# A fused graph-layer kernel: node work one step later behind the edges, SyncE's queue reordered, window loads signalled per half

## The chip, the cores and the metric

The kernel runs on one core of a Trainium2 chip. TensorE (PE), VectorE (DVE), ScalarE (ACT) and GpSimd (POOL) compute; SyncE (SP) only issues transfers and reads registers. GpSimd also issues the gathers, whose addresses come from an index tile. The metric is the device time of one execution in microseconds. The kernel before took 705.6 us (median of 3 runs, 704.37 to 707.84).

## The reference

One message-passing layer over 50,000 nodes of 128 features and 25,000 edges that are sorted by their destination:

```
h   = relu(layernorm(x))                                   # 50000 x 128
e   = [h[src], h[dst], edge_attr(32), vec[src], vec[dst]]  # 25000 x 290
msg = silu(e @ mW1 + mb1) @ mW2 + mb2                      # 25000 x 128
agg = segment_sum(msg, dst)                                # 50000 x 128
u   = silu([h, agg, vec] @ uW1 + ub1) @ uW2 + ub2
out = x + layernorm(h + u) * gamma + beta
```

## The kernel before

**Two streams in one pipeline.** The edges are worked in 49 steps of 512 (four tiles of 128), the nodes in 49 steps of 1,024 (eight tiles of 128). `run_pipeline` lets every engine walk the same list of steps; in step n an engine does its part for edges near n and for nodes near n minus `NODE_LAG` (4). Steps 0 to 3 therefore hold edge work only (with the first loads and norms of nodes), steps 4 to 48 hold both, steps 49 to 52 the last four node steps, and steps 53 and 54 finish them. `it.edge(d)` and `it.node(d)` name the edge or node step that lies d steps off. Each engine executes its own instructions in the written order; semaphores order the engines among each other.

**Edges.** GpSimd gathers the two end rows of each edge of step n (line 418, eight gathers). VectorE takes their statistics (lines 897 and 898) and computes reciprocal deviations in a chain of small operations that ends in `rstd` and `minus`. One step later ScalarE normalises the gathered rows (`norm_ends`, line 611), TensorE turns them (line 530), ScalarE copies them out (line 666), and the two coordinates of each edge are turned on TensorE (line 499), copied (line 627) and moved into `feat_t` by SyncE (line 326). Another step later TensorE sums the hidden layer (lines 487, 488, 491), ScalarE applies silu (line 619), TensorE makes the message (517, 519), ScalarE evicts it (line 643) and SyncE stores it to the tensor `msgs` in HBM (line 360).

**Nodes.** The messages of 128 nodes are a short run of rows of `msgs`, since edges are sorted. SyncE reads the first edge of each of the eight node tiles from SBUF into a register (line 351, eight reads per step) and loads a window of 112 message rows for each tile (line 376, eight loads into `msg_in`), one step ahead of their use. VectorE compares each message's destination with the node numbers and so makes a 0/1 matrix `match` (line 798, in two halves), TensorE multiplies windows by `match` into the hidden layer (line 555), ScalarE applies silu (line 697), TensorE makes the update (567, 569), VectorE takes its statistics (849), centres it (782) and two steps after the match finishes the output (813), which SyncE stores (line 342). GpSimd adds `beta` to six of eight tiles of x (line 438), and waits with that for the match of the step.

**What the window loads need.** Before them SyncE waits until a message store has landed: with a lag of 4 it is `it.edge(2 - NODE_LAG)` = `it.edge(-2)`, the very store that SyncE issued earlier in the same step (line 374). All eight loads raise one semaphore, and the first half of `match` waits for all eight.

**SyncE's order in a step** is: register reads, x load, message store, coordinates, edge indices and edge attributes (every other step), the node coordinate row, output store, window loads.

The flag `sorted_near` picks this path (`WHOLE`) on the chip; the other path, for edges that are not sorted, is not run on these inputs.

## Time and profile before

| | |
|---|---|
| median of 3 runs | 705.6 us (704.37 to 707.84) |
| profiled execution, its own time | 707.65 us |
| its span in the trace | 705.6 us |
| DVE busy | 624.5 us, 89% |
| PE busy | 613.4 us, 87% |
| ACT busy | 542.4 us, 77% |
| POOL busy | 470.8 us, 67% |
| TensorE's granted clock | 0.986 of full speed over the span |
| moved by the DMA engines | 119.07 MB, 169 GB/s |

The table's busy times are averages over stages. SyncE has no busy time in such a table: its register reads and transfer issues are not counted, and are seen only in its timeline and in the chain of waits. The run has three stages: edge steps alone (to about 60 us), 45 steps that hold both kinds of work, and node steps alone (from about 650 us).

### The profile page before, as it was taken

The numbers are of one execution on the slowest core, as the hardware profiler recorded it, in microseconds if no ns is written. First come the engines' busy times: TensorE is split into PE (matmuls) and PEld (weight loads), VectorE is DVE, ScalarE is ACT, GpSimd is POOL, SyncE is SP. The second block draws the span as 40 slices with busy tenths as digits, with TensorE's granted clock in tenths as the row PEclk, the third lists the DMA queues.
The fourth block names the chain that finished last, engine by engine and source line by source line (L and its number), as shares of the span: only waits on it lengthen the run. The fifth ranks groups of instructions, "written<-read, shape, count | busy, mean of one in ns | idle before, by whom it ended". The sixth has DMA issues, their size and how long they took to land.

```text
span 705.6 us, 17834 instructions
## 1 busy us (share of the span) xinstructions
PE 613.4 (87%) x3685; PEld 446.7 (63%) x3732; DVE 624.5 (89%) x2949; ACT 542.4 (77%) x1181; POOL 470.8 (67%) x447
## 2 busy tenths in 40 slices
PE   1478899999899899899899899899899899989972
PEld 0155676676676676676676676676676676666662
DVE  5564789989999999999999999999999999988887
ACT  1388887887888888888888888888887888888720
POOL 7775777777777677677777677677777677763200
PEclk9999999999999999999999999999999999999997
DMA  5535576566577666667577577576576577664332
GB/s 145 171 109 133 133 217 178 163 205 160 160 186 190 167 185 191 166 186 196 155 192 197 155 200 193 150 207 186 149 215 179 148 213 181 179 191 124 122 91 84
DMA packets 91988, 119.07 MB, mean 169 GB/s; under 512 B 20250, under 2 KB 65493, under 8 KB 91944
## 3 DMA queue, kind: packets, MB, share of 16 engines
q1 hardware_dynamic: 77684, 91.61, 44.1%
q0 software_dynamic: 12752, 26.57, 17.0%
q10 hardware_dynamic: 1508, 0.42, 0.3%
q8 instruction: 13, 0.21, 0.1%
q14 instruction: 31, 0.25, 0.1%
HBM read 79.63 MB, written 38.70 MB: 168 GB/s over the span
## 4 chain that ended last, share of the span: by engine, by line
SPq 44%; DMA 17%; issue 16%; DVE 10%; PE 5%; POOL 2%; ACT 2%; DVEq 0%; POOLq 0%; ACTq 0%
SPq L376 19%; DMA msgs<-msg 14%; SPq L351 14%; SPq L326 3%; DVE y_out L813 2%; SPq L334 2%; POOL ends_in L418 2%; DVE stats L849 2%; DMA ends_in<-in_rows,end_idx 1%; SPq L360 1%; DVE centred L782 1%; DMA msg_in<-msgs 1%; SPq L342 1%; DVE stats L839 1%; SPq L319 1%
## 5 line engine op out<-in xcount | busy, mean ns | idle before, releaser
L418 POOL DMA_INDIRECT ends_in<-in_rows,end_idx x392 | 382.4, 976 | 116.2 <-issue 105.1
L611 ACT ACTIVATE ends_norm<-ends_in,minus,rstd 128x128 f32<-128x128 f32 x392 | 155.6, 481 | 11.5 <-DVE minus L954 11.5
L555 PEld LDWEIGHTS ps_hid<-match,msg_in 113*128 113x128 f32 x784 | 99.1, 191 | 102.4 <-DVE match L798 77.4
L611 ACT ACTIVATE x_norm<-x_in,minus,rstd 128x128 f32<-128x128 f32 x392 | 155.5, 482 | 0.0
L555 PE MATMUL ps_hid<-match,msg_in 113*128 113x128 f32 x784 | 108.0, 281 | 39.2 <-DVE match L798 39.2
L438 POOL TENSOR_TENSOR x_beta<-x_in,beta_row 128x768 f32<-128x768 f32 x47 | 85.5, 1819 | 79.9 <-DVE match L798 58.5
L813 DVE SCALAR_TENSOR_TENSOR y_out<-centred,rstd,x_beta 128x128 f32<-128x128 f32 x392 | 128.4, 336 | 2.1 <-issue 0.3
L849 DVE BATCH_NORM_STATS2 stats<-ps_upd 128x6 f32<-128x128 f32 x392 | 110.0, 289 | 2.6 <-issue 2.6
L567 PE MATMUL ps_upd<-w_out,hidden_n 128*128 128x128 f32 x784 | 105.2, 278 | 5.2 <-DVE centred L782 5.2
L782 DVE SCALAR_TENSOR_TENSOR centred<-ps_upd,y_mean,gamma_row 128x128 f32<-128x128 f32 x392 | 107.4, 341 | 0.0
L798 DVE SCALAR_TENSOR_TENSOR match<-iota_sb,const_sb,msg_in 112x512 f32<-112x512 f32 x98 | 72.7, 750 | 39.2 <-DMA msg_in<-msgs 38.7
L839 DVE BATCH_NORM_STATS2 stats<-x_in 128x6 f32<-128x128 f32 x392 | 102.1, 284 | 0.8 <-DVE s_sq L925 0.2
L552 PE MATMUL ps_hid<-h_t,w_node 128*128 128x512 f32 x196 | 101.0, 597 | 0.0
L567 PEld LDWEIGHTS ps_upd<-w_out,hidden_n 128*128 128x128 f32 x784 | 96.5, 194 | 6.0 <-DVE centred L782 6.0
L697 ACT ACTIVATE hidden_n<-ps_hid,node_bias 128x512 f32<-128x512 f32 x98 | 65.2, 679 | 31.3 <-PE ps_hid L555 31.2
L619 ACT ACTIVATE hidden_e<-ps_e,mb_col 128x512 f32<-128x512 f32 x49 | 33.7, 688 | 63.4 <-PE ps_e L491 62.1
L897 DVE BATCH_NORM_STATS2 stats<-ends_in 128x6 f32<-128x128 f32 x196 | 54.5, 278 | 20.2 <-DMA ends_in<-in_rows,end_idx 20.1
L635 ACT ACTIVATE h_t<-ps_t,b_col 128x1024 f32<-128x1024 f32 x49 | 54.6, 1115 | 15.4 <-PE ps_t L509 11.8
L530 PE MATMUL ps_t<-const_sb,ends_norm 128*128 128x128 f32 x392 | 54.1, 283 | 10.3 <-ACT ends_norm L611 10.0
L569 PE MATMUL ps_upd<-const_sb,h_t 128*128 128x128 f32 x392 | 59.3, 274 | 0.0
L491 PE MATMUL ps_e<-feat_t,w_feat 34*128 34x512 f32 x98 | 55.9, 651 | 3.3 <-DMA feat_t<-coords 3.3
L666 ACT ACTIVATE ends_t<-ps_t 128x1024 f32<-128x1024 f32 x49 | 50.2, 1025 | 10.4 <-PE ps_t L530 10.1
(90 smaller groups left out, 789.4 us busy)
## 6 DMA issues: line engine op xcount, KB each, us to landing
x_in<-in_x_steps SPq DMA_DIRECT2D x49, 512.0 KB
out<-y_out SPq DMA_DIRECT2D x48, 512.0 KB
msg_in<-msgs SPq DMA_DIRECT2D x392, 56.4 KB
msgs<-msg SPq DMA_DIRECT2D x49, 258.0 KB
ends_in<-in_rows,end_idx POOLq DMA_INDIRECT x392
feat_t<-in_attr SPq DMA_DIRECT2D x25, 128.0 KB
feat_t<-coords SPq DMA_DIRECT2D x98, 2.0 KB
match<-in_node_vec SPq DMA_DIRECT2D x49, 4.0 KB
```

The lines of the kernel that those rows point to most:

```text
L351: firsts = [sp.value_load(first_edge[0:1, bass.ds(N_TILES * soon.n + j, 1)]) for j in range(N_TILES)]
L376: sp.dma_start(msg_in[soon.half][0:WINDOW, j, :], msgs[bass.ds(firsts[j], WINDOW), :]).then_inc(msg_loaded[soon.half], 16)
L418: nc.gpsimd.indirect_dma_start(out=dst, out_offset=None, in_=rows, in_offset=bass.IndirectOffsetOnAxis(ap=end_idx[s.slot // 2][:, s.slot % ...
L438: nc.gpsimd.tensor_tensor(x_beta[later.slot][:, 0:POOL_TILES, :], x_in[later.slot][:, 0:POOL_TILES, :], beta_row[:, :, :].broadcast_to([P, ...
L552: nc.tensor.matmul(ps_hid[:, bank], w_node[:, :], h_t[k.half][:, bank], start=True, stop=False)
L555: last = nc.tensor.matmul(ps_hid[:, cols(j)], msg_in[k.half][0:WINDOW + 1, j, 0:H], match[k.half][0:WINDOW + 1, j, :], start=False, stop=j ...
L567: nc.tensor.matmul(ps_upd[:, cols(j)], hidden_n[:, cols(j)], w_out[:, :], start=j == tiles[0], stop=False)
L611: return nc.scalar.activation(dst, source, function, bias=minus[was][:, c:c + 1], scale=rstd[was][:, c:c + 1])
L782: last = V.scalar_tensor_tensor(centred[:, j, :], ps_upd[:, j * P:(j + 1) * P], y_mean[:, j:j + 1], gamma_row[:, 0, :], ALU.subtract, ALU. ...
L813: last = V.scalar_tensor_tensor(y_out[done.half][:, j, :], centred[:, j, :], rstd[was][:, Y_AT + j:Y_AT + j + 1], x_beta[done.slot][:, j, ...
L839: last = V.bn_stats(stats[:, X_AT + j, :], x_in[n.slot][:, j, :])
L849: last = V.bn_stats(stats[:, Y_AT + j, :], ps_upd[:, j * P:(j + 1) * P])
```

## The change

`NODE_LAG` becomes 5. There is so one more step with edges alone at the start, 44 steps with both in place of 45, and one more node step behind the last edges. The awaited store is now `it.edge(-3)`, issued one step earlier.

In SyncE's list a step with node work runs: coordinates, message store, coordinate row, register reads, window loads, x load, edge indices and attributes, output store. A step without node work runs: x load, coordinates, indices and attributes, register reads, message store, row, window loads.

The window loads raise one semaphore for the first four tiles and another for the last four, and each half of `match` waits for its own.

In the steps without node work PE turns the coordinates before the hidden sum, and ACT copies the coordinates and applies silu before it normalises the ends. ACT executes one small silu on a spare column at the start. DVE splits the bias after the first step's statistics and takes the first x statistics ahead of the gathered ones; GpSimd's first `x_beta` no longer waits for a match.

```
-NODE_LAG = 4
+NODE_LAG = 5
...
-            def body(it):
-                soon, done, e = it.node(1), it.node(-2), it.edge(-2)
-                if soon and it.mode == WHOLE:
...
-                    firsts = [sp.value_load(first_edge[0:1, bass.ds(N_TILES * soon.n + j, 1)]) for j in range(N_TILES)]
...
+                def load_windows(firsts):
...
+                        if past := it.edge(2 - NODE_LAG):
+                            wait_apart(sp, msg_stored[past.slot], 16 * (past.fills4 + 1), sp_passed)
+                        for j in range(N_TILES):
+                            sp.dma_start(msg_in[soon.half][0:WINDOW, j, :], msgs[bass.ds(firsts[j], WINDOW), :]).then_inc(
+                                msg_loaded[soon.half][2 * j // N_TILES], 16)
...
+                if not k:
+                    load_ahead()
+                    if own:
+                        move_coords(own)
+                    load_pairs()
+                    firsts = find_windows()
+                    store_messages()
+                    load_row()
+                    load_windows(firsts)
+                else:
+                    if own:
+                        move_coords(own)
+                    store_messages()
+                    load_row()
+                    load_windows(find_windows())
+                    load_ahead()
+                    load_pairs()
...
-                    wait(pool, match_ready, 2 * later.n - 2)
+                    if isinstance(later.n, int) and later.n == 2:
+                        pool.wait_ge(x_beta_low_ready, 2)
+                    else:
+                        wait(pool, match_ready, 2 * later.n - 2)
...
+            act.wait_ge(fold_loaded, 16 * N_FOLD)
+            nc.scalar.activation(spare[:, :], mb2_col[:, :], ACT.Silu)
...
                 if not k:
+                    copy_coords()
+                    activate_edges()
                     norm_ends()
-                    activate_edges()
-                    copy_coords()
                     copy_ends()
...
+                    if it.mode == WHOLE:
+                        dve.wait_ge(msg_loaded[k.half][half], 16 * HALF * (k.fills2 + 1))
                     if half == 0:
-                        if it.mode == WHOLE:
-                            dve.wait_ge(msg_loaded[k.half], 16 * N_TILES * (k.fills2 + 1))
```

SyncE's queue around one even step, in the kernel before: from the last window load of a step to the first of the next.

```order
L376 DMA msg_in<-msgs 112x129
L351 TENSOR_LOAD first_edge x8
L334 DMA x_in<-in_x_steps 128x1024
L360 DMA msgs<-msg 128x516
L326 DMA feat_t<-coords 1x4x128 x2
L314 DMA end_idx<-in_ends 128x16
L319 DMA feat_t<-in_attr 32x1024
L369 DMA match<-in_node_vec 1x1024
L342 DMA out<-y_out 128x1024
L376 ISA
```

The same piece of SyncE's queue in the changed kernel (one of the first steps, which has no output to store yet).

```order
L392 DMA msg_in<-msgs 112x129
L337 DMA x_in<-in_x_steps 128x1024
L317 DMA end_idx<-in_ends 128x16
L322 DMA feat_t<-in_attr 32x1024
L329 DMA feat_t<-coords 1x4x128 x2
L368 DMA msgs<-msg 128x516
L374 DMA match<-in_node_vec 1x1024
L383 TENSOR_LOAD first_edge x8
L392 ISA
```

The x load, the indices, the attributes and (from two steps later on) the output store have moved behind the windows; coordinates and message store are first, and the register reads stand right before the window loads.

ScalarE's queue in the third step, which has edge work alone, in the kernel before.

```order
L651 ACTIVATE msg<-end_idx 128x4
L611 ACTIVATE ends_norm<-ends_in,minus,rstd 128x128 x8
L619 ACT_TABLE_LOAD
L619 ACTIVATE hidden_e<-ps_e,mb_col 128x512
L627 ACTIVATE coords<-ps_f 8x128
L666 ACTIVATE ends_t<-ps_t 128x1024
L643 ACTIVATE msg<-ps_e 128x4x128
```

The same step on ScalarE in the changed kernel.

```order
L669 ACTIVATE coords<-ps_f 8x128
L661 ACTIVATE hidden_e<-ps_e,mb_col 128x512
L693 ACTIVATE msg<-end_idx 128x4
L653 ACTIVATE ends_norm<-ends_in,minus,rstd 128x128 x8
L708 ACTIVATE ends_t<-ps_t 128x1024
L685 ACTIVATE msg<-ps_e 128x4x128
```

Coordinates and the hidden layer's silu stand ahead of the eight norms, and the table load is gone from here to the program's start.

## Rows read from the trace of the kernel before

**Rows 1.** The page: the chain of work that ended last, shares of span.

```profile
SPq 44%; DMA 17%; issue 16%; DVE 10%; PE 5%; POOL 2%; ACT 2%; DVEq 0%; POOLq 0%; ACTq 0%
```

**Rows 2.** Timeline, SyncE, two steps: start us, us, engine line, op, out<-in, count.

```profile
300.05 0.35 SPq L334 DMA_DIRECT2D x_in<-in_x_steps  x1
...
313.36 0.35 SPq L334 DMA_DIRECT2D x_in<-in_x_steps  x1
...
316.83 0.37 SPq L342 DMA_DIRECT2D out<-y_out  x1
318.61 3.87 SPq L376 DMA_DIRECT2D msg_in<-msgs  x8
326.10 0.35 SPq L334 DMA_DIRECT2D x_in<-in_x_steps  x1
```

**Rows 3.** Waits of the SP queue, 169 to 550 us: total us, times, longest.

```profile
SPq L72 <- DMA msgs<-msg: 13.9, 14, 1.6
```

**Rows 4.** Waits of all engines, 169 to 550 us.

```profile
PE ps_hid L555 <- DVE match L798: 26.0, 29, 1.4
DVE match L798 <- DMA msg_in<-msgs: 14.6, 25, 1.2
```

**Rows 5.** Timeline, VectorE's match: step 4 (both halves), steps 5 and 48 (second).

```profile
60.85 1.41 DVE L798 SCALAR_TENSOR_TENSOR match<-iota_sb,const_sb,msg_in 112x512 f32<-112x512 f32 x2 [8.29 <-DMA msg_in<-msgs]
...
73.61 0.74 DVE L798 SCALAR_TENSOR_TENSOR match<-iota_sb,const_sb,msg_in 112x512 f32<-112x512 f32 x1
...
640.04 0.74 DVE L798 SCALAR_TENSOR_TENSOR match<-iota_sb,const_sb,msg_in 112x512 f32<-112x512 f32 x1
```

**Rows 6.** Timeline, ScalarE, from one silu of the edges to the next.

```profile
637.09 0.69 ACT L619 ACTIVATE hidden_e<-ps_e,mb_col 128x512 f32<-128x512 f32 x1 [1.34 <-PE ps_e L491]
...
639.87 3.18 ACT L611 ACTIVATE ends_norm<-ends_in,minus,rstd 128x128 f32<-128x128 f32 x8
...
649.66 0.69 ACT L619 ACTIVATE hidden_e<-ps_e,mb_col 128x512 f32<-128x512 f32 x1 [1.34 <-PE ps_e L491]
```

**Rows 7.** Timeline, TensorE, the same step.

```profile
643.10 1.09 PE L530 MATMUL ps_t<-const_sb,ends_norm 128*128 128x128 f32 x8
```

**Rows 8.** Timeline, GpSimd, one step.

```profile
313.20 1.82 POOL L438 TENSOR_TENSOR x_beta<-x_in,beta_row 128x768 f32<-128x768 f32 x1 [1.37 <-DVE match L798]
...
324.19 0.95 POOL L418 DMA_INDIRECT ends_in<-in_rows,end_idx  x1 [0.30 <-DVE y_out L813]
```

**Rows 9.** Timeline, VectorE, from the ends' statistics to the next match.

```profile
315.11 0.28 DVE L897 BATCH_NORM_STATS2 stats<-ends_in 128x6 f32<-128x128 f32 x1
...
325.12 0.75 DVE L798 SCALAR_TENSOR_TENSOR match<-iota_sb,const_sb,msg_in 112x512 f32<-112x512 f32 x1
```

**Rows 10.** DMA queues (q0 gathers), 326 to 326.5 us: packets, MB, share.

```profile
q0 software_dynamic: 19, 0.01, 11.1%
```

**Rows 11.** The chain in order of time: start us, us, what.

```profile
58.76 2.07 DMA msg_in<-msgs
...
73.49 4.96 DMA ends_in<-in_rows,end_idx
...
99.71 5.30 DMA ends_in<-in_rows,end_idx
```

**Rows 12.** DMA queues (q1 is SyncE's), 104 to 105 us.

```profile
q1 hardware_dynamic: 102, 0.37, 94.1%
```

**Rows 13.** Timeline, ScalarE, the table load and step 4's message eviction.

```profile
36.36 1.28 ACT L619 ACT_TABLE_LOAD   x1
...
59.52 0.60 ACT L643 ACTIVATE msg<-ps_e 128x512 f32<-128x512 f32 x1 [1.02 <-PE ps_e L519]
```

**Rows 14.** Timeline, VectorE, node steps behind the last edges.

```profile
674.33 1.41 DVE L798 SCALAR_TENSOR_TENSOR match<-iota_sb,const_sb,msg_in 112x512 f32<-112x512 f32 x2 [3.16 <-DMA msg_in<-msgs]
...
683.01 1.42 DVE L798 SCALAR_TENSOR_TENSOR match<-iota_sb,const_sb,msg_in 112x512 f32<-112x512 f32 x2
...
691.88 2.19 DVE L813 SCALAR_TENSOR_TENSOR y_out<-centred,rstd,x_beta 128x128 f32<-128x128 f32 x8
```

More of the change, by code:

```diff
@@ L344, in body, with load_ahead, load_pairs, store_messages @@
             def body(it):
-                soon, done, e = it.node(1), it.node(-2), it.edge(-2)
-                if soon and it.mode == WHOLE:
+                soon, k, done, e, own = it.node(1), it.node(0), it.node(-2), it.edge(-2), it.edge(-1)
+                def load_ahead():
+                    if further := it.node(5):
+                        if it.begins_nodes():
+                            for n in range(further.n):
+                                load_nodes(Step(n, n, 0))
+                        load_nodes(further)
+                def load_pairs():
+                    if (s := it.edge(2)) and s.slot % 2 == 0:
+                        load_edges(s)
+                    if (s := it.edge(0)) and s.slot % 2 == 0:
+                        load_attr(s)
+                def store_messages():
+                    if not e:
+                        return
+                    wait_apart(sp, dst_copied, e.n + 1, sp_passed)
+                    wait_apart(sp, msg_ready, e.n + 1, sp_passed)
+                    sp.dma_start(msgs_v[e.n], msg[e.slot][:, :, :]).then_inc(msg_stored[e.slot], 16)
+                def load_row():
+                    if not soon:
+                        return
+                    wait_apart(sp, hidden_n_summed, 2 * soon.n - 2, sp_passed)
+                    sp.dma_start(match[soon.half][WINDOW:WINDOW + 1, :, :], coord_v[soon.n]).then_inc(coord_loaded[soon.half], 16)
+                def find_windows():
+                    if not soon or it.mode != WHOLE:
+                        return None
                     if isinstance(soon.n, int) and soon.n == 0:
@@ L361, in body @@
-                if s := it.edge(-1):
-                    move_coords(s)
-                if (s := it.edge(2)) and s.slot % 2 == 0:
-                    load_edges(s)
-                if (s := it.edge(0)) and s.slot % 2 == 0:
-                    load_attr(s)
-                if soon:
-                    wait_apart(sp, hidden_n_summed, 2 * soon.n - 2, sp_passed)
-                    sp.dma_start(match[soon.half][WINDOW:WINDOW + 1, :, :], coord_v[soon.n]).then_inc(coord_loaded[soon.half], 16)
-                if done and e:
-                    store_nodes(done)
@@ L372, in body @@
-                if soon and it.mode == WHOLE:
-                    if past := it.edge(2 - NODE_LAG):
-                        wait_apart(sp, msg_stored[past.slot], 16 * (past.fills4 + 1), sp_passed)
-                    for j in range(N_TILES):
-                        sp.dma_start(msg_in[soon.half][0:WINDOW, j, :], msgs[bass.ds(firsts[j], WINDOW), :]).then_inc(msg_loaded[soon.half], 16)
-                elif soon:
+                    return [sp.value_load(first_edge[0:1, bass.ds(N_TILES * soon.n + j, 1)]) for j in range(N_TILES)]
@@ L380, in body @@
                     sp.dma_start(agg_in[soon.half][:, :, :], table_v[soon.n]).then_inc(agg_loaded[soon.half], 16)
-                if done and not e:
+                if not k:
[15 more added lines that the diff above has]
+                    load_pairs()
+                if done:
                     if isinstance(done.n, int) and done.n == NODE_STEPS - 1:
@@ L893, in body @@
                         centre(j)
+                if nxt and it.begins_nodes():
+                    for j in range(N_TILES):
+                        x_stat(nxt, j)
                 if new:
@@ L899, in body @@
                     last.then_inc(ends_stats, 1)
-                if nxt and it.begins_nodes():
-                    for j in range(N_TILES):
-                        x_stat(nxt, j)
                 if not (new or nxt or prev):
```

63 lines of the change are left out of this document (32 added, 31 removed).

## The prediction

> **What bounds the kernel now.** The page's busy times come first and mislead: VectorE at 89% and TensorE at 87% look like the bound. The chain of work that ended last says otherwise: 44% of the span lies in SyncE's own queue and 17% in transfers, only 10% on VectorE [rows 1]. So I read SyncE's timeline. From one x load to the next it takes 13.31 us in an even step (300.05 to 313.36) and 12.74 us in an odd one (313.36 to 326.10) [rows 2]. In the even step every gap is a few hundredths of a microsecond: the queue is simply full. In the odd step, which has no index and attribute loads, the output store ends at 317.20 and the first window load comes at 318.61 [rows 2]. About 0.37 us of such a gap is register work (the same place in the even step); the other 1.04 us is the wait for the message store of the same step to land. Over 169 to 550 us, 29 steps, that wait sums to 13.9 us in 14 odd steps [rows 3].
>
> Who waits for SyncE: VectorE waits for the windows 14.6 us in these 29 steps, and TensorE waits 26.0 us for VectorE's match behind it [rows 4]. From step 5 to step 48 the second half of match moves from 73.61 to 640.04 us, 43 intervals of 13.17 us [rows 5].
>
> What a step would take without that wait, loop by loop:
> - SyncE: 381 us less 13.9 us over 29 steps is 12.66 us. Its steps alternate, 13.31 us and 12.74 - 1.04 = 11.70 us in the two shown.
> - VectorE: 381/29 = 13.14 us less 14.6/29 = 0.50 us is 12.64 us, at most.
> - ScalarE with TensorE: silu of the edges starts at 637.09, the eight norms of the ends run from 639.87 to 643.05, TensorE's transposes start at 643.10 directly behind them, and the next silu starts at 649.66 [rows 6, 7]. That ring closes in 12.57 us with no wait for a match in it, and the change leaves its order alone.
> - The gathers: GpSimd adds beta once the match is done (313.20), and issues the last of eight gathers at 324.19 [rows 8]. The last packets of the gather queue pass between 326 and 326.5 us [rows 10], 2.31 us behind that issue. VectorE needs 10.76 us from the ends' statistics to the end of the next match (315.11 to 325.87) [rows 9]. This ring spans two steps: 10.99 + 2.31 + 10.76 + 0.1 = 24.2 us, 12.1 us a step.
>
> So four rings lie at 12.1 to 12.7 us, and the kernel runs at 13.17. That is the room.
>
> **The change part by part.**
>
> *Lag 5.* The awaited store is a step older, so it was issued some 12 us before, and the slowest landing fits many times: the wait of 13.9 us in 29 steps goes. What is late next is SyncE's own list, 12.66 us, with the ScalarE ring 0.1 us under it. Rings so close add up their small disturbances, and SyncE's even steps are 0.65 us over its mean, which is covered only while the windows are early enough. I take 12.75 us. The ends are 12.57 us (the ScalarE ring alone) and 13.6 us (the gather rival below).
>
> *SyncE's new order.* Nothing is added: eight register reads, eight window loads, one x load, one store, two coordinate moves, one row and one output store per step, as before. Moved past other work are the x load (512 KB), the indices, the attributes and the output store (512 KB): they start some 8 us later against the message store. The x load has time, since VectorE reads it more than a step later. The indices are needed for the gathers of two steps later; this margin shrinks by about 5 us and I cost it at nothing, hidden by GpSimd's wait for the match; without that cover it would be some 0.5 us a step. The windows no longer queue behind 512 KB of output, worth something only where they are late. What the moved megabyte meets is the gathers' end: the slow rival.
>
> *Semaphore per half.* The first match may start four window issues earlier, half of 3.87 us [rows 2]; the second half still waits for the last. In a full pipeline VectorE's 12.64 us hides that. I count it only in the first and last steps.
>
> *The head.* The first match comes one step later, at step 5, so I compare it with step 5 before, at 73.61 us [rows 5]. It needs windows whose issue now stands behind the store of message 2, evicted in step 4. Before, this eviction ended at 60.12 [rows 13]; ScalarE's eight norms (3.18 us [rows 6]) now stand ahead of it, so 63.3. Then store and row 1.0 us, eight window loads with gaps 4.6 us, landing 2.07 us [rows 11], and 0.4 us to the second half: 71.4 us, 2.2 us less than before. Earlier statistics, the bias split behind them and GpSimd's first addition, which sat 5.6 us for a match, serve the same start. Bounds: -6 us (most of the 8.29 us that VectorE waits here [rows 5]) to +3 us.
>
> *The table load.* It takes 1.28 us between two activations of the third step [rows 13] and goes to a time when ScalarE idles; that is inside the head's bounds. The Trainium skill (ScalarE: Activation LUTs, "What ACT_TABLE_LOAD costs") gives a switch some 2.66 us with a drain; here silu follows the load at once, so the trace shows the load's 1.28 us and no drain. By the page the head would be 1.4 us shorter.
>
> *The tail.* Before, from step 48's match (640.04) to the end are 65.6 us. A node step alone takes 8.7 us (674.33 to 683.01) where VectorE waits for nothing, and 12 us where it waits 3.16 us for windows [rows 14]. Now: 12.4 us from match 48 to 49 (this step still takes x statistics), 8.2 to step 50, 10.5 to step 51 (its windows stand behind the last message store), 8.9, 8.7, then 8.2 to the output work of step 54, 7.5 for one more, 6.2 to the end as before: 70.6 us, 5.0 us more. Bounds: +1 to +8.7 us, a whole step.
>
> *Sum.* 71.4 + 43 x 12.75 (548.3) + 70.6 = 690.3 us of span, against 705.6. The profiled execution took 707.65 us, 2.05 us around its span; with the same 2.05 the changed one takes 692.3, 15.3 us less. The median before was 705.6, so I predict 690 us.
>
> **The rivals.**
>
> *R1, it stops only at the ScalarE ring.* Then 43 x 12.57 = 540.5 us, and 682 us in all. For it: 12.57 us was reached late in the run [rows 6]. Against: SyncE's mean of 12.66 us is instruction work that stays.
>
> *R2, slower: the gathers land late.* Twice early in the run the last gather took 4.96 and 5.30 us to land [rows 11], in place of 2.31. At the second, SyncE's queue held the DMA engines at 94.1% from 104 to 105 us [rows 12], while the mid-run gather lands in a quiet spell [rows 10]. The new order lets x load and output store start right behind the windows, 8 to 10 us after a match, and the last gather is issued 12 us after it. If they meet in every step, the two-step ring is 10.99 + 4.96 + 10.76 + 0.1 = 26.8 us, 13.4 a step, with 5.30 us 13.6: 43 x 13.43 + 71.4 + 70.6 = 719 us. It decides where the landing passes 3.6 us (two steps of 12.75); above 4.3 us the gain is gone. Against it: if this ring slows the kernel, SyncE is no longer the bound, is up to 3 us earlier, and its megabyte is over before the gathers end. The Trainium skill (DMA: Bandwidth & Descriptors, "Queues, rings and completion order") says that each DMA engine takes turns between the queues that hold work, a packet at a time; the 94.1% beside a late gather agrees. By it alone the cost of a meeting is bounded by the share, so it makes a later landing likely and a stopped one not.
>
> *R3, the gain is eaten.* Landings of 4 us or window issues that stretch (4.64 us is the kind seen at the start) hold a step at 13.05 us: 561 + 142 = 703 us. For it: rings this close. Against: the same queue did 3.87 us per eight windows in most steps.
>
> *R4, the wait does not go.* Excluded but for an error of reading, 1 in 50: 708 us, with the tail's cost alone.
>
> **How the numbers follow.** Forecast (685 to 698 us) 0.62, R1 0.17, R3 0.10, R2 0.09, R4 0.02. A difference of 0.5%, 3.5 us, is about what a measurement of this kernel can tell from none. Faster than 702 us are the forecast, R1 and four tenths of R3: 0.83. Within 0.5%: most of R3's rest, R4's edge: 0.08. Slower: 0.09. The range runs from 678 us (R1 with the head's good end) to 705 us (R3 whole); outside are R2, R4 and a sliver below.
>
> **What would show it.** In SyncE's timeline the gap before the windows is gone in odd steps and a pair of steps takes 25.3 to 25.5 us. Match to match 12.75 us; VectorE's wait for windows under 0.2 us a step. The ScalarE ring shows TensorE's transposes waiting for the norms. The first match at step 5 near 71 us, the last two-sided match near 620, 70 us before the end. I am wrong if VectorE's statistics wait for gathers in the middle of the run (R2), if SyncE's pair stays at 26 us (R3 or R4), or if the tail takes more than 75 us.

## The result: 0.9% slower, where 2% faster was forecast

The changed kernel takes 714.22 us (median of 12 runs, 709.62 to 716.56) beside 707.69 us for the kernel before (12 runs, 704.37 to 708.99): ratio 1.0087, 95% interval 1.0065 to 1.011. It lies outside the range of 678 to 705 us. The profiled execution took 712.72 us, its span is 710.8.

Cut at the same two places as the forecast, the second half of match of step 5 and of step 48:

| part of the span, us | before | forecast | after |
|---|---|---|---|
| head, to match of step 5 | 73.61 | 71.4 | 78.93 |
| 43 steps, one step | 566.4 (13.17) | 548.3 (12.75) | 556.9 (12.95) |
| tail | 65.6 | 70.6 | 74.9 |
| span | 705.6 | 690.3 | 710.8 |

Against before: +5.3 - 9.5 + 9.4 = +5.2 us. Against the forecast every part is worse: +7.5, +8.6, +4.3.

The page of after, busy times and the chain that ended last (it answers to [rows 1], where 44% lay in SyncE's queue):

```profile
PE 620.7 (87%) x3685; PEld 452.2 (64%) x3732; DVE 627.1 (88%) x2962; ACT 540.4 (76%) x1181; POOL 469.8 (66%) x447
DVE 29%; issue 24%; POOL 22%; PE 10%; DMA 7%; ACT 5%; SPq 2%; DVEq 1%; POOLq 0%; ACTq 0%
```

SyncE went from 44% to 2%. The bound has moved, as meant, and to VectorE and GpSimd's gathers. SyncE's timeline of after (start us, us), one step from x load to x load, against [rows 2]:

```profile
399.94 0.35 SPq L337 DMA_DIRECT2D x_in<-in_x_steps  x1
400.62 0.37 SPq L345 DMA_DIRECT2D out<-y_out  x1
401.26 1.56 SPq L329 DMA_DIRECT2D feat_t<-coords  x2
403.25 0.36 SPq L368 DMA_DIRECT2D msgs<-msg  x1
403.95 0.28 SPq L374 DMA_DIRECT2D match<-in_node_vec  x1
407.79 3.86 SPq L392 DMA_DIRECT2D msg_in<-msgs  x8
412.03 0.35 SPq L337 DMA_DIRECT2D x_in<-in_x_steps  x1
```

What SyncE waits for most between 169 and 550 us, against [rows 3] (us in total, times, longest):

```profile
SPq L72 <- ACT msg L685: 1.3, 5, 0.3
```

and what VectorE waits for most in the same stretch, against [rows 4]:

```profile
DVE stats L943 <- DMA ends_in<-in_rows,end_idx: 7.2, 8, 1.5
```

The wait for the message store (13.9 us) is gone, and so is VectorE's for the windows (14.6 us). New is VectorE's wait for gathered rows. The two matches that bound the middle, against [rows 5]:

```profile
78.93 0.75 DVE L841 SCALAR_TENSOR_TENSOR match<-iota_sb,const_sb,msg_in 112x512 f32<-112x512 f32 x1 [1.09 <-DMA msg_in<-msgs]
...
635.86 0.74 DVE L841 SCALAR_TENSOR_TENSOR match<-iota_sb,const_sb,msg_in 112x512 f32<-112x512 f32 x1
```

**The head.** ScalarE in step 3 of after and into step 4:

```profile
49.56 3.17 ACT L653 ACTIVATE ends_norm<-ends_in,minus,rstd 128x128 f32<-128x128 f32 x8
54.79 1.02 ACT L708 ACTIVATE ends_t<-ps_t 128x1024 f32<-128x1024 f32 x1 [2.06 <-PE ps_t L568]
56.92 0.60 ACT L685 ACTIVATE msg<-ps_e 128x512 f32<-128x512 f32 x1 [1.11 <-PE ps_e L557]
...
62.51 0.69 ACT L661 ACTIVATE hidden_e<-ps_e,mb_col 128x512 f32<-128x512 f32 x1 [1.77 <-PE ps_e L529]
```

and TensorE beside it:

```profile
52.78 1.97 PE L568 MATMUL ps_t<-const_sb,ends_norm 128*128 128x128 f32 x8 [3.95 <-ACT ends_norm L653]
54.97 1.92 PE L557 MATMUL ps_e<-w_fold,hidden_e 128*128 128x128 f32 x8 [0.22 <-issue]
...
57.67 2.05 PE L525 MATMUL ps_e<-ends_t,w_src 128*128 128x512 f32 x2 [0.56 <-ACT msg L685]
59.51 1.91 PE L526 MATMUL ps_e<-ends_t,w_dst 128*128 128x512 f32 x2
61.35 1.12 PE L529 MATMUL ps_e<-feat_t,w_feat 34*128 34x512 f32 x2
```

Read as a ring: norms (49.56), transposes (52.78), the sums of the message, which stand behind the transposes on TensorE (54.97), the eviction of the message (56.92), the next hidden sum, which is made in the same tile `ps_e` and waits for that eviction (57.67 to 62.47), silu (62.51), and only then, since silu now stands ahead of them on ScalarE, the next norms. They start at 63.19, 13.6 us after the last. ScalarE's copy of the transposed rows (54.79 to 55.81) is not a link of this ring: it ended 1.9 us before the hidden sum began, although the expectation of old_head below names it as one.

The first four silus of the edges (steps 2 to 5) are 13.6, 13.6 and 13.6 us apart in after, and 9.6, 9.0 and 14.7 us in the kernel before: 7.6 us more in these three steps. The same work is longer here than in the full pipeline (transposes 1.97 us, 1.09 in [rows 7]), since the granted clock is at its lower level for most of this time. Windows of 5 us in after, the columns being length, busy times, granted clock, DMA share and GB/s:

```profile
35.00:40.00 5.00, 1.05 (x5) 0.85 (x5) 4.39 (x28) 3.85 (x10) 3.78 (x5) 0.75 0.34 82
40.00:45.00 5.00, 4.44 (x17) 3.32 (x16) 0.23 (x2) 1.77 (x3) 3.78 (x5) 0.50 0.25 59
```

and in before:

```profile
35.00:40.00 5.00, 3.58 (x15) 3.09 (x16) 3.76 (x23) 4.39 (x8) 3.78 (x5) 1.00 0.23 53
40.00:45.00 5.00, 2.42 (x8) 0.95 (x6) 2.00 (x9) 4.49 (x13) 4.09 (x4) 1.00 0.46 107
```

TensorE was busy 1.05 of 5 us ahead of a stretch at 0.50 (1.2 GHz) in after; in before 3.58 of 5, and the clock stayed at 1.00 (2.4 GHz). So the ring idles the engine, and what follows runs at the lower clock. The clock is not what makes the head late, though: windows_first, with the old order and a head 11 us shorter, also has a stretch at 0.50 (45 to 50 us). What the clock adds to the ring was not measured by itself.

**The meeting of transfers.** In the step shown above x load and output store go out at 399.94 and 400.62. The last gather is issued at 402.44. Windows of 1 us show the DMA engines full behind it:

```profile
404.00:405.00 1.00, 1.00 (x8) 0.76 (x7) 1.00 (x5) 1.00 (x4) 0.83 (x1) 1.00 1.01 400
405.00:406.00 1.00, 1.00 (x8) 0.76 (x8) 1.00 (x5) 1.00 (x4) 0.99 (x1) 1.00 0.75 289
```

the chain gives that gather's landing

```profile
402.44 4.65 DMA ends_in<-in_rows,end_idx
```

and VectorE is late by 0.95 us:

```profile
407.11 0.29 DVE L943 BATCH_NORM_STATS2 stats<-ends_in 128x6 f32<-128x128 f32 x1 [0.95 <-DMA ends_in<-in_rows,end_idx]
```

In [rows 8, 10] the last packets passed 2.31 us behind the issue, in a quiet spell; by its semaphore, as here, that gather landed 2.51 us behind it.

**The tail.** SyncE of after, behind the last edge step,

```profile
661.36 0.37 SPq L368 DMA_DIRECT2D msgs<-msg  x1
661.83 0.30 SPq L374 DMA_DIRECT2D match<-in_node_vec  x1
665.58 4.13 SPq L392 DMA_DIRECT2D msg_in<-msgs  x8
```

and VectorE's match that waits for these windows:

```profile
669.18 0.75 DVE L841 SCALAR_TENSOR_TENSOR match<-iota_sb,const_sb,msg_in 112x512 f32<-112x512 f32 x1 [2.96 <-DMA msg_in<-msgs]
```

The windows stand behind the last message store although they don't need it: 13.6 us from match to match for that step, where 10.5 was forecast.

### The profile page after: what moved, and what is told of

It is laid out like the page before. It is cut to its first block, busy times and chain, and to the rows that moved or that the text cites. A ratio compares the mean times of both kernels' runs of the same rounds, so it can differ in the third digit from the quotient of the medians.

```text
span 710.8 us, 17950 instructions
## 1 busy us (share of the span) xinstructions
PE 620.7 (87%) x3685; PEld 452.2 (64%) x3732; DVE 627.1 (88%) x2962; ACT 540.4 (76%) x1181; POOL 469.8 (66%) x447
## 4 chain that ended last, share of the span: by engine, by line
DVE 29%; issue 24%; POOL 22%; PE 10%; DMA 7%; ACT 5%; SPq 2%; DVEq 1%; POOLq 0%; ACTq 0%
POOL ends_in L453 22%; DVE y_out L856 7%; DMA ends_in<-in_rows,end_idx 6%; DVE stats L892 5%; DVE centred L825 3%; ACT ends_norm L653 3%; DVE stats L882 3%; DVE stats L944 2%; PE ps_t L568 2%; DVE stats L943 2%; DVE match L841 1%; PE ps_e L525 1%; PE ps_e L557 1%; PE ps_e L526 1%; SPq L392 1%
## 5 line engine op out<-in xcount | busy, mean ns | idle before, releaser
L841 DVE SCALAR_TENSOR_TENSOR match<-iota_sb,const_sb,msg_in 112x512 f32<-112x512 f32 x98 | 72.8, 749 | 23.6 <-DMA msg_in<-msgs 22.4
L661 ACT ACTIVATE hidden_e<-ps_e,mb_col 128x512 f32<-128x512 f32 x49 | 33.7, 688 | 72.3 <-PE ps_e L529 72.3
L708 ACT ACTIVATE ends_t<-ps_t 128x1024 f32<-128x1024 f32 x49 | 50.2, 1024 | 14.1 <-PE ps_t L568 13.4
L568 PEld LDWEIGHTS ps_t<-const_sb,ends_norm 128*128 128x128 f32 x392 | 46.3, 148 | 21.8 <-ACT ends_norm L653 21.2
```

The costliest lines, as they stand in the source:

```text
L568: last = nc.tensor.transpose(ps_t[:, cols(t)], ends_norm[own.half][:, t, :], ident)
L841: V.scalar_tensor_tensor(match[k.half][0:WINDOW, tiles, :], iota[0:WINDOW, tiles, :], const[0:WINDOW, bass.ds(C_BASE + N_TILES * k.n, 1)], ...
```

## The experiments

Kernels were run at several occasions, each beside the kernel before. At four of them (windows_first, gathers_early, transfers_later, lag4_old_head_c) the kernel before took its usual 707.72 to 709.94 us. At the others it took 1011 to 1032 us; what differs there is told in the last section, and those runs are read for their sign and for one interval of the head alone.

**windows_first**: both orders of the edges-only steps undone on ScalarE and TensorE, and the windows put ahead of the message store.

```
  (ScalarE, steps without node work)
-     copy_coords()
-     activate_edges()
      norm_ends()
+     activate_edges()
+     copy_coords()
...
  (TensorE, steps without node work)
-     turn_coords()
      begin_messages()
+     turn_coords()
...
  (SyncE, every step)
-     store_messages(); load_row(); load_windows(...)
+     load_row(); load_windows(...); store_messages()
```

> The changed kernel with the edges-only steps of ScalarE and TensorE ordered as before, and with row, register reads and windows ahead of the message store of the same step on SyncE, in every step (with a lag of five the windows don't need that store). In the changed kernel the first windows stood behind the store of a message evicted at 70.56 us, and those of the step after the last edge step behind one evicted at 661.26. If the kernel before takes 700 to 710 us here: theory A (head and tail are what the change lost) expects the second half of match of step 5 at 66 to 71 us, 12.95 us a step, a tail of 71 to 72 us, in all 696 to 702 us. Rival B (the first windows are late because the steps are, so their place does nothing) expects 71 to 73 us for the head and 707 us in all. If the kernel before takes over 1000 us here, with each instruction 0.7 us in stretches of each step, neither is told apart, and only the sign against the kernel before is read.

Measured: 701.03 us (before 707.72), ratio 0.9896 (0.9861 to 0.9931). Head 67.7, 13.03 us a step, tail 71.3. Theory A holds for head and tail: -11.2 and -3.7 us against after. Two edits were made at once; which of them did the head is read from this trace. ScalarE in its step 4:

```profile
51.82 3.18 ACT L653 ACTIVATE ends_norm<-ends_in,minus,rstd 128x128 f32<-128x128 f32 x8 [0.67 <-DVE minus L996]
54.91 0.67 ACT L661 ACTIVATE hidden_e<-ps_e,mb_col 128x512 f32<-128x512 f32 x1
...
58.88 0.60 ACT L685 ACTIVATE msg<-ps_e 128x512 f32<-128x512 f32 x1 [0.79 <-PE ps_e L557]
```

and SyncE in the same step:

```profile
60.76 0.28 SPq L374 DMA_DIRECT2D match<-in_node_vec  x1
61.34 4.31 SPq L392 DMA_DIRECT2D msg_in<-msgs  x8
65.85 0.37 SPq L368 DMA_DIRECT2D msgs<-msg  x1
```

Norms wait for VectorE's `minus`, not for silu: the ring is open. The message was evicted at 59.48, before SyncE came to the row at 60.76, so a store ahead of the row would have waited for nothing and cost its own 0.4 us. So the order on ScalarE and TensorE made the head's loss, and lag4_old_head below bears it out: there the windows stand behind the store, the lag is four, and the head is 68.7. The old order is the only edit that both kernels share. The windows' place made the tail's 3.7 us: the step behind the last store takes 9.2 us from match to match in place of 13.6, and the first step of the tail 1.4 us more than in after. The middle did not gain, against the 12.95 us expected: VectorE's waits for gathers are larger (17.8 us between 80 and 620, 13.7 in after).

**old_head**: the order of ScalarE and TensorE alone undone.

> The changed kernel, with the steps that have edges only (steps 1 to 4) ordered on ScalarE and TensorE as before: norms of the ends, then silu, then the coordinates; the sums for the hidden layer ahead of the turned coordinates. Theory A (the new order of these two engines closes a serial ring of 13.6 us in the head, norms, transposes, copy, hidden sum, silu, norms): the second half of match of step 5 comes at 71 to 73 us in place of 78.93, the middle stays at 12.95 us a step and the tail at 74.9, so the time falls by 6 to 8 us, from 714 to 707. Rival B (the head is late for another reason: the step more of lag, SyncE's order, or TensorE's lower clock of itself): match of step 5 stays between 77 and 80 us, and the time within 1.5 us of 714.

The same kernel ran three more times:

> The kernel of old_head again, on another occasion, because in the first one the kernel before itself took 1011 us and every engine's sequencer needed 0.7 us for each instruction in stretches of 8 to 10 us a step. If the kernel before takes 700 to 710 us here: theory A (the new order of ScalarE and TensorE in the edges-only steps closes a serial ring) expects the second half of match of step 5 at 71 to 73 us and 707 us in all; rival B (the head is late for another reason) expects 77 to 80 us and 712 to 716 us in all.

> The kernel of old_head once more, since the same comparison could only be read for its sign where the kernel before took over 1000 us. Theory A (the new order of ScalarE and TensorE in the edges-only steps closes a serial ring of 13.6 us): with windows_first at 67.71 us for the second half of match of step 5, this one, whose windows stand behind the message store, comes at 70 to 73 us, and 706 us in all (704 to 708). Rival B (the ring costs nothing, and only the windows' place behind the store made the head late): 77 to 79 us and 712 to 714 us in all.

> The kernel of old_head, alone in its call. Theory A (the new order of ScalarE and TensorE in the edges-only steps closes a serial ring of 13.6 us a step): with windows_first at 67.71 us for the second half of match of step 5, this one, whose windows stand behind the message store, comes at 70 to 73 us, and 704 to 708 us in all. Rival B (the ring costs nothing, and only the windows' place behind the store made the head late): 77 to 79 us and 712 to 714 us in all.

Measured, each time where the kernel before took over 1000 us: 0.985 (0.9795 to 0.9905), 0.9817, 0.9832 and 0.9889 of it. The total can't decide between the theories, and neither can the head: it is 91 to 93 us in these four, and the first silu already comes at 54.5 to 55.1 us, where windows_first has it at 33.7. What still tells the orders apart is the distance of the first silus of the edges. In old_head's first run

```profile
54.52 0.66 ACT L661 ACTIVATE hidden_e<-ps_e,mb_col 128x512 f32<-128x512 f32 x1
62.02 0.69 ACT L661 ACTIVATE hidden_e<-ps_e,mb_col 128x512 f32<-128x512 f32 x1
```

they are 7.5 us apart, and the first two such distances are 7.5 to 10.2 us in all four runs. With the new order, in the three runs of lag4_rest, they are 13.6 to 22.0 us, and in the two of old_sync, which has it too, 12.4 to 16.2. What the old order alone gives in microseconds at usual speed was not measured.

**gathers_early**: windows_first, and GpSimd's addition ahead of the gathers waits for the first half of match.

```
-    wait(pool, match_ready, 2 * later.n - 2)
+    wait(pool, match_ready, 2 * later.n - 3)
```

> windows_first with one change: GpSimd's addition of beta, which stands ahead of the eight gathers of the next step, waits for the first half of match in place of the second, so that it and the gathers behind it may begin up to 1.4 us earlier. Theory A (VectorE's own list takes 12.6 us a step in windows_first, and the other 0.36 to 0.52 us a step there are its waits for the last gather, which hang on GpSimd's wait for the match): VectorE's waits for the gathers fall below 0.15 us a step, the step goes from 13.03 to 12.7 us, and with windows_first at 701 us the time is 686 to 691 us. Rival B (the gathers land late because x load and output store hold the DMA engines, whenever they are issued): the waits stay at 0.3 us a step or more and the time is within 3 us of windows_first. Rival C (SyncE's list, 12.9 us with its small waits, sets the step once VectorE is free): VectorE waits for windows in place of gathers, 12.9 us a step, 695 to 697 us. If the kernel before takes over 1000 us here, only the sign is read.

Measured: 701.21 us, ratio 0.989 (0.9852 to 0.9928), 13.05 us a step: no change. Rival B. VectorE's waits for gathers went from 17.8 to 15.1 us between 80 and 620 us, and the last gather lands later behind its issue (median 4.37 us, 4.18 in windows_first). The halves of match are 0.74 us apart, and of that 0.52 us are lost again, since the addition takes longer when it runs beside the second half. This kernel:

```profile
421.97 2.33 POOL L476 TENSOR_TENSOR x_beta<-x_in,beta_row 128x768 f32<-128x768 f32 x1 [1.07 <-DVE match L841]
```

windows_first, where it starts behind it:

```profile
330.26 1.81 POOL L476 TENSOR_TENSOR x_beta<-x_in,beta_row 128x768 f32<-128x768 f32 x1 [0.86 <-DVE match L841]
```

**transfers_later**: windows_first, with x load and output store between coordinates and row.

```
      move_coords(own)
+     load_ahead(); store_nodes(done)
      load_row(); load_windows(...); store_messages()
-     load_ahead()
      load_pairs()
-     store_nodes(done)
```

> windows_first with SyncE's x load and output store issued behind the coordinate moves and ahead of the row, in place of behind the windows: the order in the ring of a step is kept but for these two, which come 4 to 6 us later against the gathers. In windows_first they are issued 1 to 3 us before the last gather, the DMA engines are full from 446 to 449 us, 2 to 3 us behind their issue at 442.63 and 443.32, and VectorE's statistics then wait for a gather issued at 445.67. Theory A (the collision of these 1024 KB with the last gather makes the waits of 0.36 to 0.52 us a step, and VectorE's own list is 12.6 us): VectorE's waits for the gathers fall under 0.15 us a step, 12.65 to 12.75 us a step, and the time is 10 to 15 us under windows_first's 701 us, 686 to 691. Rival B (the gathers take 4.2 us from issue to statistics by themselves, whatever else flows, and GpSimd's list sets the step): no change of the waits, 699 to 703 us. Rival C (the megabyte now stands before the windows, so VectorE waits for these in their place, as in the kernel before): waits for windows of 0.3 us a step or more, 13.1 to 13.3 us a step, 703 to 712 us. If the kernel before takes over 1000 us here, only the sign is read.

Measured: 721.52 us (before 709.94), ratio 1.0175 (1.0147 to 1.0203), head 67.3, 13.52 us a step, tail 70.6. Rival C, and more than it allowed. VectorE's waits between 80 and 620 us in windows_first

```profile
DVE stats L943 <- DMA ends_in<-in_rows,end_idx: 17.8, 24, 2.4
```

and in this kernel:

```profile
DVE match L843 <- DMA msg_in<-msgs: 29.5, 39, 1.9
DVE stats L945 <- DMA ends_in<-in_rows,end_idx: 2.5, 4, 1.3
```

The waits for gathers all but vanish, but that alone does not show the collision, since a longer step leaves each gather more time. The landings do better: with x load and output store issued behind the last gather, its landing has a median of 3.53 us, 4.18 in windows_first. What made the step longer is SyncE itself (chain of this kernel):

```profile
SPq 57%; issue 19%; PE 9%; DVE 7%; POOL 4%; DMA 2%; ACT 2%; DVEq 0%; POOLq 0%; ACTq 0%
```

It did not wait for a message store, and for coordinates only once (1.7 us). Its queue is full, and one instruction in it is longer. The chain in order of time: the row load, then register reads:

```profile
422.48 0.27 SPq L374
...
422.89 1.51 SPq L383
...
424.51 0.27 SPq L383
```

The first of the eight reads takes 1.42 us (median of 22 steps between 200 and 500 us, 0.86 to 1.72), with the megabyte issued just ahead of it. In windows_first it takes 0.45 us, with the same row load ahead of it, and in the kernel before, where the reads stand ahead of x load and store, 0.44; the other seven take 0.27 us in all three. So the eight reads take 4.10 us in place of 3.10, and SyncE's list of 12.66 us becomes one of some 13.6 (an estimate from these two numbers; measured 13.52 a step). Why the read is longer there is not shown. This order with the reads ahead of the x load was not run, and it is what would test theory A.

**lag4_old_head**: the change with a lag of four and the old order of the edges-only steps; its third run (lag4_old_head_c) fell where the kernel before takes its usual time.

```
-NODE_LAG = 5
+NODE_LAG = 4
...
-PIPELINES = {WHOLE: (8, 44, ...
+PIPELINES = {WHOLE: (9, 45, ...
...
  (ScalarE and TensorE as in windows_first, SyncE as in the change)
```

> The changed kernel with a lag of four and with ScalarE and TensorE in the edges-only steps ordered as before: what is left of the change is SyncE's order, the semaphore per half, the early silu table and VectorE's early statistics. By the theories A of both parts the gain of the middle (0.22 us a step, 9.5 us) stays, the tail is 65 to 67 us as before, and the head is at or up to 3 us under the one before (second half of match of step 5 at 70 to 74 us): 695 to 698 us in all, 1.2 to 1.7% under the kernel before. If SyncE then waits for the store in each step, 715 us or more; if the head needs the new order with this lag, 702 to 705 us.

> The kernel of lag4_old_head once more, where the kernel before takes 700 to 710 us: the change with a lag of four and with ScalarE and TensorE in the edges-only steps as before. Against old order and lag of the kernel before it keeps SyncE's order, which puts the row and eight register reads (4.2 us) between the message store and the windows. Theory A (these reads cover the landing of the store, so the lag of five buys nothing in the middle and costs a step at the end): no wait of SyncE for the store, 12.95 to 13.05 us a step as in windows_first, second half of match of step 5 at 66 to 72 us, tail from match of step 48 65 to 67 us, in all 691 to 699 us, likeliest 695, under windows_first's 701. Rival B (the store lands later than the reads cover, and the wait stands in every step): 13.4 us a step or more, 710 us or more. If the kernel before takes over 1000 us here, only the sign is read.

> The kernel of lag4_old_head a last time, where the kernel before takes 700 to 710 us. In the changed kernel SyncE goes from the message store to the first window in 4.5 to 4.6 us without a wait; in the kernel before, where it waited for the store in every second step, the same stretch took 4.33 to 4.58 us, which is the landing. Theory A (the new order covers the landing by itself, the lag of five buys nothing in the middle and costs a step at the end): no wait of SyncE for the store beyond 0.1 us a step, 12.95 to 13.05 us a step, second half of match of step 5 at 66 to 72 us, tail from the match of step 48 65 to 67 us, 691 to 699 us in all, likeliest 695. Rival B (the store lands later than the reads cover): 13.4 us a step or more, 710 us or more. If the kernel before takes over 1000 us here, only the sign is read.

Measured in the third: 698.22 us (before 707.77), ratio 0.9854 (0.9819 to 0.989), head 68.68, 13.09 us a step, tail 64.9. Theory A, though the step and the total are a little over the 13.05 and the likeliest 695 us. SyncE's waits between 80 and 620 us:

```profile
SPq L72 <- ACT coords L669: 9.1, 12, 2.5
SPq L72 <- ACT msg L685: 4.6, 12, 0.4
SPq L72 <- DMA msgs<-msg: 0.7, 2, 0.5
```

The awaited store is that of the same step again, and costs 0.7 us in 41 steps (22.4 us in before). SyncE shows why; store, row, then reads that last till the windows:

```profile
424.17 0.35 SPq L368 DMA_DIRECT2D msgs<-msg  x1
424.87 0.28 SPq L374 DMA_DIRECT2D match<-in_node_vec  x1
428.91 4.00 SPq L392 DMA_DIRECT2D msg_in<-msgs  x8
```

The eight register reads cover the landing. The lag of five buys 0.06 us a step (windows_first, 13.03) to 0.14 us (after, 12.95), 3 to 6 us over 43 steps, about what executions of one kernel differ by (709.6 to 716.6 us in after), and costs 6.4 us in the tail against windows_first, 10.0 against after. This is the fastest version run, 1.5% under the kernel before; the interval of windows_first (0.9861 to 0.9931) overlaps its own. Its first two runs, where that took over 1000 us, gave 0.9898 and 0.9885 of it.

**lag4_rest**: the whole change, with a lag of four. **lag5_alone**: the kernel before, with a lag of five and nothing else. **old_sync**: the whole change, with SyncE's instructions in the order of before.

> The changed kernel with a lag of four steps: all the rest of the change, with the message store awaited in the step that issues it. Theory A (the eight register reads that now stand between the message store and the windows, with the row load some 3.9 us, cover the landing of the store, so that the lag isn't needed): no wait of SyncE for the store, or under 0.3 us a step, 12.95 us a step in the middle, a tail of 65 to 67 us after step 48, in all 703 to 707 us. Rival B (the store lands later than that, and the wait is in every step now, with no other transfer issued meanwhile): 0.7 us a step or more, 13.4 us a step and over, in all 722 us or more.

> The kernel of lag4_rest again. If the kernel before takes 700 to 710 us here: theory A (the register reads cover the landing of the message store, the lag isn't needed) expects 12.95 us a step, no wait of SyncE for the store, a tail of 65 to 67 us, 703 to 707 us in all; rival B (a wait of 0.7 us or more in every step) expects 13.4 us a step and 722 us or more.

> The kernel of lag4_rest once more, where the kernel before takes 700 to 710 us. Theory A (eight register reads between the message store and the windows cover the store's landing, so the lag isn't needed for the middle): 12.95 us a step, no wait of SyncE for the store, tail 65 to 67 us, 703 to 707 us in all. Rival B (a wait of 0.7 us or more in every step): 13.4 us a step, 722 us or more.

> The kernel before, with the lag of five steps alone (old order of SyncE, of the edges-only steps, one semaphore for the windows, silu table late). Theory A (the wait for the message store goes by the lag alone, and VectorE's own list of 12.7 us with SyncE's of 12.66 us then sets the step): 12.75 to 12.95 us a step, head 72 to 76 us at step 5, tail 74 to 76 us; in all 697 to 708 us, likeliest 703. Rival B (the saving in the middle needs SyncE's new order too, because the output store of 512 KB ahead of the windows makes them late): 13.1 us a step and more, in all over 712 us.

> The kernel of lag5_alone again. If the kernel before takes 700 to 710 us here: theory A (the lag alone takes the wait away, VectorE's own list of 12.7 us then sets the step) expects 12.75 to 12.95 us a step, a head of 72 to 76 us, a tail of 74 to 76 us, 703 us in all; rival B (windows behind the output store come late) expects 13.1 us a step or more and over 712 us.

> The kernel of lag5_alone once more, where the kernel before takes 700 to 710 us. Theory A (the lag alone takes the wait for the store away, and VectorE's own list with its small waits for the gathers then sets the step): 12.85 to 13.0 us a step, head 72 to 76 us, tail 74 to 76 us, 705 us in all (700 to 709). Rival B (windows behind the output store come late, and the order of SyncE is needed): 13.1 us a step or more, over 712 us.

> The changed kernel with SyncE's instructions in the order of before (register reads, x load, message store, coordinates, indices and attributes, row, output store, windows), the lag of five kept. Theory A (VectorE's own list of 12.7 us a step is the bound and the later landing of the last gather adds 0.25 us, which comes from x load and output store behind the windows): the gathers land in 2.3 us again, VectorE's waits for them go from the middle, 12.7 us a step, 9 to 11 us less than the changed kernel's middle, in all 702 to 706 us if the head stays as it is. Rival B (SyncE's order is needed: windows behind the output store come late): VectorE waits for the windows 0.2 us a step or more, 12.95 to 13.2 us a step, in all 713 to 722 us.

> The kernel of old_sync once more, where the kernel before takes 700 to 710 us. Theory A (VectorE's list of 12.7 us a step is the bound, and its small waits for the gathers, 0.25 us a step, come from x load and output store behind the windows): the last gather lands in 2.3 us again, 12.7 to 12.8 us a step, head and tail as in the changed kernel, 705 us in all (702 to 708). Rival B (the waits for the gathers don't come from the order, or SyncE's old order makes the windows late in their place): 12.95 to 13.2 us a step, 713 us or more.

All fell where the kernel before took 1011 to 1032 us. lag4_rest: 0.9817 (0.9733 to 0.99), 0.9689 and 0.9739 of it. lag5_alone: 1.0286 (1.0223 to 1.0349), 1.025 and 1.0128. old_sync: 1.0193 (1.0117 to 1.0269) and 1.0102. In every pair the order of the change went with faster, and the lag alone was slower than before. That agrees with the runs at usual speed, but the sizes don't carry over, and neither the lag alone nor the old order of SyncE with the lag of five was measured there. The semaphore per half, the early silu table and VectorE's earlier statistics were never taken out one by one: what each of them gives is not known.

## Why the prediction was wrong

**Right.** SyncE was the bound; its wait for the store went; the waits for windows went with it; R4 is out. A cost of a longer lag in the tail was foreseen (5.0 us; measured 6.4, windows_first's 71.3 less lag4_old_head's 64.9).

**The head, the step that failed.** The prediction let the eight norms stand once ahead of one eviction ("so 63.3"). The reorder costs in every edges-only step, since the norms of a step now wait for the silu of the same step, and that silu, over hidden sum, eviction, message and transposes, for the norms of the step before: 13.6 us a step. Measured, the eviction ended at 71.16 and the head came at 78.93 in place of 71.4. That "the change leaves its order alone", as the prediction has it of ScalarE and TensorE, holds only for the steps that have node work. That the edit closes a ring was to be read from the kernel: silu ahead of norms on ScalarE, transposes ahead of the message on TensorE, and message and hidden sum in one tile. With the old order the head is 67.7 to 68.7: the rest of the change gained 5 to 6 us there, which the reorder turned into a loss of 5.3.

**The middle, a term mis-sized.** The forecast took SyncE's 12.66 us as next and 12.75 as the mean. VectorE is next. Its waits between 80 and 620 us, per step, taken off the step:

| | step | waits, gathers | waits, windows | rest | landing of the last gather, median |
|---|---|---|---|---|---|
| before | 13.17 | 0.10 | 0.43 | 12.64 | 2.56 |
| after | 12.95 | 0.33 | 0.01 | 12.61 | 3.85 |
| windows_first | 13.03 | 0.43 | 0 | 12.60 | 4.18 |
| gathers_early | 13.05 | 0.36 | 0.02 | 12.67 | 4.37 |
| transfers_later | 13.52 | 0.06 | 0.74 | 12.72 | 3.53 |
| lag4_old_head | 13.09 | 0.49 | 0 | 12.60 | 3.79 |

The landing is the time from the issue of a step's last gather to the last increment of its semaphore, of 39 to 42 gathers in each trace.

The rest hardly moves: VectorE's own list, 12.6 us, for which the prediction had 12.64 as the most. What the sum of 12.75 left out is the gathers' landing, R2's mechanism, which had 0.09. R2 priced it as 4.96 us in every step (13.4 us); R3, with landings of 4 us and 13.05 us a step, came nearest and had 0.10. In after all 40 gathers took over 3.1 us (mean 3.98), and 13 of them made VectorE wait. R2's own sum with 3.98 us, (10.99 + 3.98 + 10.76 + 0.1) / 2, is 12.92 us; measured 12.95.

The argument against R2 was that SyncE would be up to 3 us earlier and its megabyte over in time. The landing does depend on that distance, but SyncE got nowhere near it: it now waits for ScalarE's coordinates and messages (7.5 and 3.2 us between 80 and 620 us). Mean landing by when the x load is issued against the last gather:

| x load issued | kernel | gathers | mean landing |
|---|---|---|---|
| behind the gather | before | 37 | 2.67 |
| up to 1.0 us ahead of it | before | 4 | 4.56 |
| up to 2.5 us ahead | after | 11 | 4.71 |
| 2.5 to 3 us ahead | after | 13 | 3.87 |
| 3 us ahead or more | after | 16 | 3.56 |
| 5 us ahead or more | windows_first | 2 | 2.58 |

This is the evidence for the collision within one kernel. The four late ones of before and seven of the eleven of after lie in the first 181 us; the other four, between 299 and 595 us, take 4.78 us on the mean, so it is not the start of the run that makes them late. The last line rests on two gathers alone. The Trainium skill ("DMA: Bandwidth & Descriptors", "Queues, rings and completion order") has each DMA engine take turns, a packet at a time, between the queues that hold work for it. By that a gather beside full queues is later, not stopped; 4.65 us in place of 2.51 at a DMA share of 1.01 agrees.

**The tail.** +9.4 us where 5.0 was forecast. 6.4 us are the node-only step itself (windows_first less lag4_old_head, which is 0.7 us under the kernel before); 3.7 us are the windows behind a store that they don't need (after less windows_first). That place was seen in the prediction and given 10.5 us; it took 13.6. The first step of the tail took 13.4 us where 12.4 was forecast.

## What to carry to other kernels

A wait that a longer lag removes may as well be covered by work of the same queue put between the store and its readers: here eight register reads of SyncE, which had to be done anyway, did it, while the lag cost 6.4 us at the end. When several rings lie within 0.1 us of each other, removing one wait gives a fraction of it: price the next ring with its waits for transfers, and ask what the moved transfers now meet, landings and register reads both. And edits to the filling steps of a pipeline are worth a ring analysis of their own, by engine order and by shared tiles: what they cost recurs in each of these steps.

## What the runs showed of the hardware

**GpSimd beside VectorE.** The 128x768 addition takes 1.81 us when it starts behind the match and 2.33 us when 0.66 us of a match (two inputs in SBUF) runs beside it. The Trainium skill ("GPSIMD Engine Reference", "1. Specifications") states that GpSimd's way to SBUF is shared with VectorE's instructions that have two SBUF inputs; the 0.52 us agrees.

**A register read behind a megabyte of transfers.** The first of SyncE's eight reads takes 0.44 to 0.45 us in the kernel before and in windows_first, and 1.42 us in transfers_later, where x load and output store are issued just ahead. The cause stays open.

**At some occasions every kernel takes over 1000 us.** At five of nine the kernel before took 1011 to 1032 us. In those traces ScalarE, VectorE and TensorE stand idle for some microseconds in each step, while gathers are in flight. VectorE in lag4_rest:

```profile
505.96 0.18 DVE L996 SCALAR_TENSOR_TENSOR minus<-s_add,rstd 128x24 f32<-128x24 f32 x1 [1.09 <-DVE rstd L994]
510.26 0.30 DVE L892 BATCH_NORM_STATS2 stats<-ps_upd 128x6 f32<-128x128 f32 x1 [4.12 <-remote]
```

It waits 1.09 us for its own result and 4.12 us for sums that TensorE had made by 503.2 us. In the same stretch ScalarE stands idle for 5.78 us and TensorE for 3.56, while GpSimd issues its gathers 1.25 us apart as elsewhere. The operations themselves are as long as elsewhere. SyncE's register instructions, which follow each other in some 0.08 us otherwise, came 0.7 us apart from 501 to 510 us. The cause stays open; that instructions reach these engines slowly is only argued.
